# A cross-attention and mixture-of-experts kernel: the way from the token loop to the first table tile and the end rewritten, four blank tails stored by ScalarE, the experts' table worked out ahead of the small tiles'

## What is computed

```
x = x + cross_attention(context, layernorm(x))
h = layernorm(x)
logits = h @ Wr                                 # 9 experts
cw = weights of the two largest, else 0
gate = silu(h @ Wg[e]); hidden = gate * (h @ Wu[e])
out = x + sum over e of cw[e] * (hidden @ Wd[e])
```

## Time and profile before

| | us |
|---|---|
| runs | 816.67, 819.35, 820.24 |
| median | 819.35 |
| profiled execution | 819.96 |
| its span, first to last instruction | 818.2 |
| PE busy in it | 792.1 |
| DVE, ACT, POOL busy | 664.9, 623.3, 390.6 |

### The profile page before, as it was taken

One profiled execution on the slowest core, in us unless ns is written; L12 is line 12 of the kernel. 1 busy time (PEld: TensorE's weight loads), 2 busy tenths in 40 slices (PEclk: granted clock), 3 DMA queues, 4 the chain that ended last, 5 costly groups with the idle time before them and its releaser, 6 DMA issues.

```text
span 818.2 us, 19725 instructions
## 1 busy us (share of the span) xinstructions
PE 792.1 (97%) x6021; PEld 755.4 (92%) x6021; DVE 664.9 (81%) x1620; ACT 623.3 (76%) x1958; POOL 390.6 (48%) x534
## 2 busy tenths in 40 slices
PE   7999999999999999998999999999999999999994
PEld 6966899999999999888999999999999999999994
DVE  6677798888889888888678888788887878878882
ACT  5578898889889888744777887777787877778772
POOL 1021387688778767772344333334434343334443
PEclk9999999999999999999999999999999999999997
DMA  8265801401310020636475274455656556373312
GB/s 300 65 169 153 258 27 35 149 28 40 112 65 34 27 92 28 200 110 183 104 208 143 45 218 87 110 128 147 187 150 162 142 149 161 77 230 78 52 22 26
DMA packets 78060, 96.14 MB, mean 117 GB/s; under 512 B 10695, under 2 KB 65155, under 8 KB 77955
## 3 DMA queue, kind: packets, MB, share of 16 engines
q1 hardware_dynamic: 64515, 76.98, 30.8%
q0 software_dynamic: 13440, 17.90, 12.2%
HBM read 109.19 MB, written 30.23 MB: 170 GB/s over the span
## 4 chain that ended last, share of the span: by engine, by line
PE 88%; DVE 4%; ACT 3%; DVEq 1%; DMA 1%; issue 1%; SPq 1%; POOL 0%
PE banks L351 25%; PE banks L352 24%; PE banks L353 24%; PE banks L1415 4%; PE banks L1395 2%; PE banks L1581 2%; PE banks L1429 2%; ACT prob L1091 1%; DVEq L1631 1%; PE banks L1369 1%; PE banks L1343 1%; PE banks L1381 1%; DMA tok<-expert_in 1%; DMA wkv_sb<-in_L_xattn_Wkv 1%; PE banks L1553 0%
## 5 line engine op out<-in xcount | busy, mean ns | idle before, releaser
L351 PE MATMUL banks<-tok_t_hi,wgt_hi 128*128 128x256 f32 x704 | 199.7, 284 | 2.0 <-issue 1.6
L353 PE MATMUL banks<-tok_t_hi,wgt_lo 128*128 128x256 f32 x704 | 197.9, 281 | 0.0
L352 PE MATMUL banks<-tok_t_lo,wgt_hi 128*128 128x256 f32 x704 | 197.8, 281 | 0.0
L991 POOL DMA_INDIRECT result<-res,tok_id x72 | 127.7, 1774 | 137.8 <-ACT res L1226 115.0
L1091 ACT ACTIVATE prob<-banks,row_min 128x77 f32<-128x77 f32 x512 | 161.5, 374 | 2.3 <-DVE row_min L1798 2.3
L351 PEld LDWEIGHTS banks<-tok_t_hi,wgt_hi 128*128 128x128 f32 x704 | 134.3, 191 | 3.6 <-issue 3.5
L352 PEld LDWEIGHTS banks<-tok_t_lo,wgt_hi 128*128 128x128 f32 x704 | 133.5, 190 | 0.0
L353 PEld LDWEIGHTS banks<-tok_t_hi,wgt_lo 128*128 128x128 f32 x704 | 133.5, 190 | 0.0
L1091 ACT ACTIVATION_READ_ACCUMULATOR prob<-banks,row_min 128x1 f32 x512 | 130.7, 258 | 0.0
L351 PE MATMUL banks<-wgt_hi,hid_hi 128*128 128x256 f32 x360 | 105.0, 292 | 0.6 <-DVE hid_hi L2114 0.6
L353 PE MATMUL banks<-wgt_hi,hid_lo 128*128 128x256 f32 x360 | 101.9, 283 | 0.0
(11 more groups left out here) (274 smaller groups left out, 2218.7 us busy)
## 6 DMA issues: line engine op xcount, KB each, us to landing
wgt<-in_L_ffn_Wg SPq DMA_DIRECT2D x29, 704.0 KB
wgt<-in_L_ffn_Wu SPq DMA_DIRECT2D x29, 640.0 KB
wgt<-in_L_ffn_Wd SPq DMA_DIRECT2D x29, 640.0 KB
tok<-expert_in SPq DMA_DIRECT2D x32, 258.0 KB
spare_wgt<-in_L_ffn_Wg SPq DMA_DIRECT2D x9, 704.0 KB
spare_wgt<-in_L_ffn_Wu SPq DMA_DIRECT2D x9, 640.0 KB
spare_wgt<-in_L_ffn_Wd SPq DMA_DIRECT2D x9, 640.0 KB, 6.9
valmat_f<-valmat_dram SPq DMA_DIRECT2D x4, 1197.0 KB, 6.2
```

The source lines that it names most:

```text
L351: nc.tensor.matmul(to, a[0], b[0], start=first, stop=False)
L352: nc.tensor.matmul(to, a[0], b[1], start=False, stop=False)
L353: return nc.tensor.matmul(to, a[1], b[0], start=False, stop=last)
L991: nc.gpsimd.indirect_dma_start(out, bass.IndirectOffsetOnAxis(ap=tok_id[:, t % NOTES, a:a + 1], axis=0), res[i][:, a, :], None, compute_op ...
```

## The change

All five queues are rewritten between the loop's last steps and tile 3 (the first table tile), and three of them in the last tile. The parts:

- **PE, tile 2**: `down(1)` stands ahead of `tok_turn(3)`, where it stood behind it.
- **PE, last tile**: `down(NT-2)` stands between the two halves of `gate_up(NT-1, 1)`, so 12 matmuls of the unit follow it. In the final `down`, the products on the last unit's high part wait for that part alone.
- **ACT, last tile**: `round_down` and `res_move(NT-2)` stand ahead of `silu(NT-1, 1)`.
- **DVE**: `table_experts` and `table_rows` follow `hid_rest(0, 2)` directly, `tok_rest(2)` and `hidden(1, 1)` come behind them. `single_segments` and `single_rows` move into tile 2, behind `hidden(2, 2)`. DVE's order in the last tile is unchanged: `hidden`, `hid_rest` of unit 1, `rest_down`, `hidden` of unit 2.
- **Tails**: ACT stores four of the nine, two behind `silu(0, 2)` and two behind `silu(1, 2)`; SP stores five.
- **Loop's tail**: at s = T, DVE does `all_logits` and `softmax_inv` ahead of `prob_rest`, ACT the last exponentials first and the first tile's rounding ahead of the last group's; PE turns the last group of probabilities inside `attend`, behind its first group; POOL issues one scatter behind a `divide`; `ranks(T-1)` follows the whole of `gate_up(0, 2)`.
- **Step 2**: PE's wait for the values is split in two, one before `turn_probs` and one before `attend`.

The allocation of the tables is moved to another place of SBUF, and is left out here.

```diff
@@ -717,7 +716,7 @@
             sp.wait_ge(tok_noted, 1)
             load_tokens(2)
             sp.wait_ge(tail_row_made, 1)
-            for e in range(E):
+            for e in range(SCALAR_TAILS, E):
 
                 blocks = WB if e == E - 1 else 1
                 row = sp.value_load(tail_row[0:1, e:e + 1], min_val=0, max_val=E * REGION - W)
...
+                if s == T:
+                    scatter(s - 5, c - 5)
                 if has(s, 4):
...
@@ -1225,6 +1228,32 @@
                     act.wait_ge(down_done, t + 1 + (a if t == NT - 1 else 0))
                     nc.scalar.activation(res[i][:, a, :], result_bank(t, a), ACT.Copy, scale=tok_gate[:, t % NOTES, a:a + 1]
                                          ).then_inc(res_ready, 1)
+
+            def last_step(t):
+
+                own = weights_of(t)
+                silu(t, 0)
+                hid_round(t, 0)
+                round_down(t, own)
+                res_move(t - 1)
+                for u in range(1, UNITS):
+                    silu(t, u)
+                    hid_round(t, u)
+
+            def last_early_step(t):
+
+                src = weights_of(t + 1)
+                silu(t, 0)
+                round_pieces(t + 1, 0, src)
+                hid_round(t, 0)
+                silu(t, 1)
+                round_pieces(t + 1, 1, src)
+                tok_move(t + 1)
+                hid_round(t, 1)
+                act.wait_ge(last_stored, 16)
+                res_move(t - 1)
+                silu(t, 2)
+                hid_round(t, 2)
 
             def pair_step(t):
 
...
+                act.wait_ge(blank_made, 2)
+                act.wait_ge(tail_row_made, 1)
+                for e in range(e0, e1):
+                    row = act.value_load(tail_row[0:1, e:e + 1], min_val=0, max_val=E * REGION - W)
+                    nc.scalar.dma_start(expert_in[bass.ds(row, P), :], blank[:, 0, :]).then_inc(tails_stored, 16)
+
+            store_tails(0, SCALAR_TAILS // 2)
             hid_round(0, 2)
             silu(1, 0)
             hid_round(1, 0)
             silu(1, 1)
             tok_move(2)
             silu(1, 2)
+            store_tails(SCALAR_TAILS // 2, SCALAR_TAILS)
             hid_round(1, 1)
             hid_round(1, 2)
             res_move(0)
-            for t in range(2, NT):
-                if t == EARLY:
-                    act.wait_ge(fresh_ready, 1)
-                    act.wait_ge(pads_zeroed, 1)
-                    act.wait_ge(sums_stored, 16 * (B + 1))
+            last_early_step(EARLY - 1)
+            act.wait_ge(fresh_ready, 1)
+            act.wait_ge(pads_zeroed, 1)
+            act.wait_ge(sums_stored, 16 * (B + 1))
+            for t in range(EARLY, NT - 1):
                 if is_pair(t):
                     pair_step(t)
                 else:
                     single_step(t)
...
 
             def step(s, c):
                 if s == 2:
-                    for moved in val_moved:
-                        pe.wait_ge(moved, VALS // 2)
+                    pe.wait_ge(val_moved[0], VALS // 2)
                 if has(s, 2):
...
                         pe.wait_ge(att_added, s - 2)
                     for g in range(NG):
                         if (s - 2) % TB == 0:
                             pe.wait_ge(valmat_split, (s - 2) // TB * len(VAL_CHUNKS) + 2 + g)
                         mm = attend(s - 2, c - 2, g)
+                        if s >= T and not g:
...
             tok_turn(1)
-            gate_up(0, 2, between=lambda: ranks(T - 1))
+            gate_up(0, 2)
+            ranks(T - 1)
 
...
                     inner(1, 0, FC - 2)
+                    pe.wait_ge(hid_hi, UNITS_TO[t + 1])
+                    for a in range(blocks):
+                        for x in w:
+                            nc.tensor.matmul(to[a], h[a][0][:, FC - 2, :], x[:, FC - 2, :], start=False, stop=False)
                     pe.wait_ge(hid_ready, UNITS_TO[t + 1])
                     for a in range(blocks):
-                        inner(a, FC - 2, FC - 1)
+                        nc.tensor.matmul(to[a], h[a][1][:, FC - 2, :], w[0][:, FC - 2, :], start=False, stop=False)
                         last_inner(a).then_inc(down_done, 1)
                     return
...
+
+                gate_up(t, 0)
+                gate_up(t, 1, between=lambda: down(t - 1))
+                gate_up(t, 2)
+
             def single_step(t):
...
             down(0)
-            for t in range(2, NT):
+            for u in range(UNITS - 1):
+                gate_up(2, u)
+            down(1)
+            tok_turn(EARLY)
+            gate_up(2, UNITS - 1)
+            for t in range(EARLY, NT - 1):
                 if is_pair(t):
                     pair_step(t)
                 else:
                     single_step(t)
+            last_step(NT - 1)
             down(NT - 1)
 
         @block.vector
...
                     find_most()
+                if s == T:
+                    all_logits(s - 3, c - 3)
+                    softmax_inv(s - 1, c - 1)
...
 
+            def last_early_step(t):
+
+                src = weights_of(t + 1)
+                hidden(t, 0)
+                rest_pieces(t + 1, 0, src)
+                hid_rest(t, 0)
+                hidden(t, 1)
+                rest_pieces(t + 1, 1, src)
+                tok_rest(t + 1)
+                hid_rest(t, 1)
+                hidden(t, 2)
+                single_segments()
+                hid_rest(t, 2)
+                single_rows()
+
             def drain():
 
                 add_attention(T - 2)
...
             hid_rest(0, 2)
-            tok_rest(2)
-            settle()
-            hidden(1, 1)
             table_experts()
             table_rows()
+            tok_rest(2)
+            hidden(1, 1)
             dve.wait_ge(sums_stored, 16 * (B + 1))
             hid_rest(1, 0)
             table_slots()
             hidden(1, 2)
             hid_rest(1, 1)
-            single_segments()
             hid_rest(1, 2)
-            single_rows()
+            zero_pads(1).then_inc(pads_zeroed, 1)
             settle()
-            zero_pads(1).then_inc(pads_zeroed, 1)
-            for t in range(EARLY - 1, NT):
+            last_early_step(EARLY - 1)
+            for t in range(EARLY, NT):
                 if is_pair(t):
                     pair_step(t)
                 else:
```

More of the change, by code:

```diff
@@ L82 @@
 SPARE = 5 * W
+SCALAR_TAILS = 4
 ROWS = E * REGION + SPARE
@@ L563, in val_banks, with inner_vals, end_vals @@
             return banks[:, first:first + 2, 0:DE]
[L565 to L567 removed]
+        def inner_vals(s):
+            return range(SOON_VALS + 4 * s, SOON_VALS + 4 * s + 2) if s < 2 else ()
+        def end_vals(s):
+            return range(SOON_VALS + 4 * s + 2, SOON_VALS + 4 * s + 4) if s < 2 else ()
         def result_bank(t, a):
@@ L941, in step @@
                     gate_sum(s - 3, c - 3)
-                if has(s, 4):
+                if has(s, 4) and s != T - 1:
                     scatter(s - 4, c - 4)
@@ L1115, in step @@
                     nc.scalar.activation(row_sum[0][:, 1:2], eps[:], ACT.Silu)
-                if has(s, 1) and s > 1:
+                if has(s, 1) and 1 < s < T:
                     softmax_exp(s - 1, c - 1, 2)
@@ L1486, in step @@
                         turn_probs(s - 2, c - 2, g)
+                if s == T:
+                    tok_turn(0)
                 if s == T + 1:
@@ L1504, in step @@
                                 pe.wait_ge(mat_lo, MATS)
-                            for m in late_vals(s)[:LATE_VALS // 2]:
+                            for m in inner_vals(s):
                                 val(m)
-                elif has(s, 2):
-                    turn_probs(s - 2, c - 2, NG - 1)
-                if s == T:
-                    tok_turn(0)
                 if has(s, -1):
@@ L1873, in step @@
                     softmax_min(s, c, 0)
-                for m in late_vals(s)[:1]:
+                for m in inner_vals(s)[:1]:
                     val_move(m)
@@ L1878, in step @@
                         val_rest(0, g)
-                if has(s, 3):
+                if has(s, 3) and s < T:
                     all_logits(s - 3, c - 3)
@@ L1887, in step @@
                     softmax_min(s, c, 1)
-                    for m in late_vals(s)[1:LATE_VALS // 2]:
+                    for m in inner_vals(s)[1:]:
                         val_move(m)
@@ L1900, in step @@
                     zn_rest(s, c)
-                for m in late_vals(s)[LATE_VALS // 2:]:
+                for m in end_vals(s):
                     val_move(m)
@@ L1919, in table_ends @@
             def table_ends():
+                for i in range(2):
+                    dve.wait_ge(scattered[i], 32 * (T // 4))
                 nc.vector.tensor_copy(next_row[:], bank[7][:, 32:32 + E])
```

71 lines of the change are left out of this document (35 added, 36 removed).

## The result

The changed kernel takes 820.2 us (median of 20 runs, 819.53 to 822.47) against 819.03 us before (20 runs); the ratio is 1.0023, 95% interval 1.0016 to 1.0031. The profiled execution took 821.79 us, its span is 820.1. Before, they were 819.96 and 818.2. The two profiles differ by 1.8 us, the runs by 1.9 us by their ratio (1.2 us by the medians), so the profiles can be read against each other.

A forecast was written before the change was run, and what follows sets the result against it. PE was taken as the bound, busy 97% of the span. Terms 0 + 0.2 - 3.5 + 2.0 = -1.3 us gave 818.7 from the profiled 819.96, or 818.1 from the median 819.35; range 814.0 to 821.5.

The forecast's parts named there:

- within 0.5%: Whole kernel: the measured time can't be told from no change, the bound being 4.1 us; chance 0.79.
- The handoff: `tok_turn(2)` to `tok_turn(4)`: `down(1)` covers PE's wait for rows, clock stays full, `gate_up(3, 0)` starts earlier; -4.7 us.
- The give-back: Before `gate_up(4, 0)`: PE waits for DVE, delayed by the small tiles' table of 4.65 us behind `hidden(2, 2)`; +1.3 us.
- The end: Last tile: PE waits 2.6 us before the final `down` for DVE's `rest_down`, behind the later unit 1; +2.0 us.
- the clock falls at the new wait: Rival: behind PE's idle 2.6 us before the final `down`, 34 matmuls run slow, 3.1 us lost, 821.2; chance 0.12.
- The loop's tail: Steps from s = T: the second group's turn inside `attend` puts two matmuls on PE's path; +0.2 us, bounds -2.2 and +0.6.
- the queue that releases PE keeps its sum: Loop's tail: DVE's operations only change places, none leaves, so PE's waits of about 2.2 us are not recovered.
- Step 2: Split wait starts the turns up to 1.3 us earlier, but `attend` still waits for the values; 0, bounds 0 to -1.3.
- I take the turn alone: Loop's tail: only the two matmuls of the group's turn inside `attend`, 0.2 us, are counted.

The follow-up runs named there:

- b3: The changed kernel with all nine blank tails stored by SP and none by ACT; 821.11 us, ratio 1.0021.
- a4: The changed kernel with `single_segments` on DVE directly behind `hidden(2, 0)`, `single_rows` left in place; 817.55 us, ratio 0.9979.
- a1: The changed kernel with the last tile's order on PE and ACT as before, the split last products kept; 817.99 us, ratio 0.9986.
- a2: The changed kernel with `rest_down` ahead of `hidden` of unit 1 on DVE in the last tile; 817.96 us, ratio 0.9989.
- a3: The changed kernel with 20 useless matmuls on PE between `gate_up(39, 2)` and the final `down`; 819.96 us, ratio 1.0012.
- c1: The changed kernel run again without an edit, a second look at its waits; 821.83 us.
- c2: The changed kernel run again without an edit, a third look at its waits; 819.57 us.
- b1: The changed kernel with the loop's tail (steps T to T + 1, `drain`, `ranks`) in the order of the kernel before; 820.67 us, ratio 1.0021.
- b2: The kernel before with one edit on PE, `down(1)` ahead of `tok_turn(3)`; 819.04 us, ratio 0.9994.

## Why the prediction was wrong

The range (814.0 to 821.5) and "within 0.5%" held the measured 820.2. The sign did not: -1.3 us was forecast against the median and +1.2 measured, +1.9 by the ratio. Point by point:

- **The handoff, -4.7**: right, -4.6, and by the steps given: no wait, full clock, `gate_up(3, 0)` at 385.78 where 385.5 was said. One step of it was right for the wrong reason. The tails on ACT were to let SP follow the table; b3 shows no worth in them.
- **The give-back, +1.3**: mechanism right (a4), the term mis-sized. In the profile it is +2.1: the idle time was 1.93, and counted between the starts of the matmuls the wait took 2.1. The sum left out the register read behind `single_rows`, 0.77 us, which before lay beside DVE's work; 1.3 and 0.77 make the 2.1. The clock fell behind this wait in 4 of 8 executions, and the eight phases lie 3.2 above the kernel before on the average.
- **The end, +2.0**: mechanism right, a wait of 2.42 us for `rest_down` where 2.6 was said (a1, a2, a3). The size is off by the clock alone. It costs 3.5 where the clock falls, 4 of 6 executions.
- **The rival "the clock falls at the new wait"** (chance 0.12) is what happened. I priced it at 34 matmuls, 3.1 us; 16 were slow, 1.5 us, as behind the wait before the change. And I gave it one place, where it has two. The same wait at the end, 2.49 us, is followed by a fall in c1 and by none in c2. The Trainium skill, "TensorE: Matmul & The Clock Gate", "What's actually happening", says that the monitor that sets the clock runs freely and does not start with the kernel, so that the point where the clock changes varies. That is told there of the rise at a kernel's start; c1 and c2 show the like for a fall. My evidence against, two waits of 1.0 and 1.3 us without a fall, said nothing on 2.4.
- **The loop's tail, +0.2**: +0.6 (b1); the bound held. The step "the queue that releases PE keeps its sum" failed: DVE's operations keep their sum, but one of them, moved forward in `drain`, waits 0.38 us for ACT, and DVE's queue is 0.6 us late behind it. The rows of `tok_turn(0)`, which the text named, were late too, and that wait hardly sets the phase.
- **Step 2, 0**: right. Two waits of 0.7 and 0.8 stand where one of 1.35 stood, and nothing was won to 84 us beyond -0.3, less than executions differ by.

Added up: 0.4 (loop) + 0.8 (give-back) + 0.4 (to turn 39) + 0.1 + 1.5 (clock at the end) + 0.1 (handoff) - 0.3 (up to 84) make 3.0; with the forecast's -1.3 that is +1.7, and the profiles differ by +1.8. Three steps failed. The sum took the two new waits at their length and put the clock behind them at nothing: 1.5 us here. The 4.65 us of the give-back left out the 0.77 us of the register read. And "I take the turn alone" in the loop's tail, since DVE's queue did not keep its time: 0.4 us. The clock is half of the miss in this pair of profiles only. In the timed runs it is less: the eight at a mean clock of 0.996 have a median of 820.0, 1.0 above the kernel before, where 1.3 less was forecast. The profiled execution before happens to lie 0.9 us above the median of its 20 runs; where that comes from is open. The 0.4 us to turn 39 are within what executions differ by: this phase is 378.31, 377.99 and 378.00 in the changed kernel's own three profiles, and a wait of 0.21 us at 588 in the first is all that the timeline shows.

## What to carry to other kernels

When work is moved behind a wait, the idle time that it leaves on its own engine is where the next thing should go: DVE stood idle for 2.67 us at the handoff and 4.38 us at the end, right beside the operations that PE then waited for. Moving `down` on PE without moving `rest_down` on DVE turned a hidden operation into a wait. An operation that is moved forward can itself wait for another engine, and then everything behind it on its queue is late: the sum of a queue's durations does not show that. And PE's waits of 1.9 to 2.5 us had a second price here, which comes in some executions only; one profile shows it or doesn't, and comparing phases between several is what separates it.

## What was not expected of the hardware

The clock's fall is a matter of the execution: of 8 waits of 1.9 to 2.3 us, 4 were followed by about 3.4 us at 1.2 GHz (1.5 us lost); of 6 of 2.4 to 2.5 us at the end, 4 were followed by 1.2 GHz too, and so was the 2.40 us in b2. A wait of the same length filled with 20 useless matmuls (a3) was not, but neither were two of the six that were not filled, so one execution of a3 does not show that filling helps. A table read into a register on DVE cost 0.77 us once nothing covered it (the changed kernel and a4).
